# The second half of v's projection among the attention's small products, in chunks 0 to 2 of a sequence

## What is computed

```python
q = relu(split_heads(x @ Wq)) + EPS      # x normalized; 16 heads of 64
k = relu(split_heads(x @ Wk)) + EPS
v = split_heads(x @ Wv)
context = cumsum(einsum('bhnd,bhne->bhnde', k, v), axis=2)
D_inv = 1.0 / einsum('bhnd,bhnd->bhn', cumsum(k, axis=2), q)
attn = einsum('bhnd,bhnde,bhn->bhne', q, context, D_inv)
x = x + attn @ Wo + bo
x = x + down(silu(gate(norm(x))) * up(norm(x)))   # three products with values rounded to an FP4 grid
```

## Time and profile before

| | |
|---|---|
| median of three runs | 1596.24 us (1595.92 to 1596.44) |
| time of the profiled execution | 1595.75 us |
| its span, first to last instruction | 1593.8 us |
| TensorE matmuls, busy | 1574.3 us, 99% of the span |
| VectorE / ScalarE / GpSimd, busy | 1118.9 / 673.1 / 480.5 us |
| granted clock of TensorE, mean | 1.000 of full speed |

### The profile page before, as it was taken

The page is one execution under the profiler, slowest core; times in us unless marked ns, Lnnn a source line. Parts: engine busy times, 40 slices in busy tenths (PEclk is TensorE's granted clock), DMA queues, the critical chain, the costliest instruction groups (busy, mean ns, idle before and its releaser), DMA issues.

```text
span 1593.8 us, 55490 instructions
## 1 busy us (share of the span) xinstructions
PE 1574.3 (99%) x24464; PEld 1483.8 (93%) x24464; DVE 1118.9 (70%) x2438; ACT 673.1 (42%) x1281; POOL 480.5 (30%) x706
## 2 busy tenths in 40 slices
PE   8999999999999999999999999999999999999998
PEld 6889999999999999999999999999999999999998
DVE  8886766676766667666667666676666766666767
ACT  5444344344444434444444443434434444443433
POOL 4332223222233222332232333222322323332233
PEclk9999999999999999999999999999999999999999
DMA  4100000000000000000000000000000000000000
GB/s 161 32 2 16 15 15 6 15 12 16 15 6 15 12 16 16 9 12 15 13 16 15 5 16 12 16 15 15 6 15 12 16 15 6 15 12 16 9 6 18
DMA packets 22013, 26.82 MB, mean 17 GB/s; under 512 B 1808, under 2 KB 20752, under 8 KB 21776
## 3 DMA queue, kind: packets, MB, share of 16 engines
q1 hardware_dynamic: 21776, 23.27, 4.7%
HBM read 14.88 MB, written 8.39 MB: 15 GB/s over the span
## 4 chain that ended last, share of the span: by engine, by line
PE 92%; DVE 4%; issue 2%; DMA 1%; ACT 0%; POOL 0%; SPq 0%; DVEq 0%; POOLq 0%
PE bank L496 65%; PE bank L760 3%; PE bank L629 3%; PE bank L664 3%; PE bank L618 3%; PE bank L805 3%; PE bank L580 3%; PE bank L700 3%; PE bank L727 1%; PE bank L747 1%; PE bank L778 1%; PE bank L602 1%; PE bank L506 1%; DMA qkT<-in_L_attn_Wk 1%; PE bank L739 0%
## 5 line engine op out<-in xcount | busy, mean ns | idle before, releaser
L1380 POOL TENSOR_SCALAR qkT<-qkT 128x512 f32<-128x512 f32 x256 | 190.3, 751 | 267.5 <-ACT qkT L1011 267.3
L1011 ACT ACTIVATE qkT<-bank 128x512 f32<-128x512 f32 x256 | 153.0, 599 | 275.4 <-PE bank L496 223.3
L496 PE MATMUL bank<-xT_hi,wqk_hi 128*128 128x256 f32 x1024 | 213.4, 289 | 0.0
L496 PE MATMUL bank<-xT_hi,wqk_lo 128*128 128x256 f32 x1024 | 203.1, 279 | 0.0
L496 PE MATMUL bank<-xT_lo,wqk_hi 128*128 128x256 f32 x1024 | 203.1, 279 | 0.0
L1350 POOL TENSOR_TENSOR rstd<-var,minus_half 128x1 f32<-128x1 f32 x64 | 35.6, 556 | 430.9 <-DVE var L1664 430.9
L496 PEld LDWEIGHTS bank<-xT_hi,wqk_hi 128*128 128x128 f32 x1024 | 155.2, 188 | 3.4 <-DVE wqk_lo L1467 0.2
L496 PEld LDWEIGHTS bank<-xT_lo,wqk_hi 128*128 128x128 f32 x1024 | 156.0, 188 | 0.0
L496 PEld LDWEIGHTS bank<-xT_hi,wqk_lo 128*128 128x128 f32 x1024 | 155.9, 188 | 0.0
L1467 DVE TENSOR_TENSOR hqT_lo<-bank,hqT_hi 128x512 fp32r<-128x512 f32 x120 | 63.8, 553 | 119.6 <-ACT hqT_hi L1087 119.6
L1467 DVE TENSOR_TENSOR attnT_lo<-bank,attnT_hi 128x512 fp32r<-128x512 f32 (+1 forms) x128 | 88.1, 689 | 60.8 <-ACT attnT_hi L1078 60.4
(11 more groups left out here) (213 smaller groups left out, 3945.5 us busy)
## 6 DMA issues: line engine op xcount, KB each, us to landing
x_in<-in_L_attn_x SPq DMA_DIRECT2D x32, 256.0 KB, 2.8
out<-out_sb SPq DMA_DIRECT2D x64, 128.0 KB, 1.7
qkT<-in_L_attn_Wq SPq DMA_DIRECT2D x1, 1024.0 KB, 8.6
qkT<-in_L_attn_Wk SPq DMA_DIRECT2D x1, 1024.0 KB, 10.7
probs<-in_L_attn_Wv SPq DMA_DIRECT2D x1, 512.0 KB, 3.6
k_tok<-in_L_attn_Wv SPq DMA_DIRECT2D x1, 512.0 KB, 6.5
attn<-in_L_attn_Wo SPq DMA_DIRECT2D x1, 512.0 KB, 12.0
x<-in_L_attn_Wo SPq DMA_DIRECT2D x1, 512.0 KB, 13.0
```

The lines of the kernel that those rows point to most:

```text
L496: at = pe.matmul(dst, lhs_at(kt), rhs_at(kt), start=first and kt == 0, stop=last and kt == k_tiles - 1)
L1011: act.activation(flat(qkT[:, 2 * m:2 * m + 2, :]), bank[bank_of["qk", c, n]][:], ACT.Relu).then_inc(qk_relu, 1)
L1380: pool.tensor_scalar(at, at, QK_EPS, 1.0, ALU.add, ALU.mult).then_inc(qk_ready, 1)
```

## The change

`project_v` and `evacuate_v` get a parameter that says which halves they work on, and `attend` a call that it makes behind the second part of L664, ahead of the queries by state. In chunks 0 to 2 the first half of v is projected where both were, and the second in that new place. In chunk 3 both stay where they were. ScalarE copies the second half behind its square of x. The table of banks is the same. Line numbers behind `attend` are 2 higher in TensorE's program, 4 higher in ScalarE's (5 behind its copy of v) and 5 higher in GpSimd's and VectorE's.

```diff
-            def project_v(b, c, u, t):
+            def project_v(b, c, u, t, parts):
 
-                for n in range(2):
+                for n in parts:
...
-            def attend(b, c, g, u, between):
+            def attend(b, c, g, u, between, amid=None):
...
                         if first:
                             last.then_inc(late_keys_done, 1)
+                if amid:
+                    amid()
...
-                project_v(b, c, u + 1, c % 2)
                 if c < CHUNKS - 1:
-                    attend(b, c, g, u, between)
+
+                    project_v(b, c, u + 1, c % 2, (0,))
+                    attend(b, c, g, u, between, lambda: project_v(b, c, u + 1, c % 2, (1,)))
                 else:
+                    project_v(b, c, u + 1, c % 2, range(2))
                     last_attend(b, c, g, u)
...
-                evacuate_v(c, u + 1, c % 2, 1 - c // 2)
+                evacuate_v(c, u + 1, c % 2, 1 - c // 2, parts=(0,))
                 if g == 2:
                     square_weights(6)
                 if g == 3:
                     square_weights(7)
                 if normed and g != 2:
                     square_x(g - 1)
+                evacuate_v(c, u + 1, c % 2, 1 - c // 2, parts=(1,))
```

More of the change, by code:

```diff
@@ L999, in flat, with evacuate_v @@
                 return t.rearrange("p j t -> p (j t)")
-            def evacuate_v(c, u, t, par, first=0):
-                for n in range(2):
+            def evacuate_v(c, u, t, par, first=0, parts=range(2)):
+                for n in parts:
                     act.wait_ge(v_projected, 4 * u + 2 * t + n + 1)
```

## The result

| | median (runs) | profiled execution | its span |
|---|---|---|---|
| before | 1596.08 us (4 runs, 1594.64 to 1596.44) | 1595.75 us | 1593.8 us |
| changed | 1616.57 us (4 runs, 1615.36 to 1620.28) | 1615.36 us | 1613.4 us |

The ratio of the runs is 1.0138, with a 95% interval of 1.0126 to 1.0150: 22 us. The two medians of the table lie 20.5 us apart, and the two profiled executions 19.6 us; what follows goes by the ratio unless it says otherwise. On the 1596.24 us from which I forecast, the ratio gives 1618.3 us, where I had said 1614 with 1609 to 1617.5. The direction and the boundaries were right, the size 18% too small, and the range ended 0.8 us too low.

A forecast was written before the change was run, and what follows sets the result against it. TensorE's own program was taken as the bound. Boundaries of 0.36 us in 47 chunks, less a wait removed, plus waits brought and the start, made 18.5 us over 1595.75: 1614 us, range 1609 to 1617.5.

The forecast's parts named there:

- the boundaries: v's wide block between two small blocks costs 0.36 us beyond its products, once in each of 47 chunks.
- the range: 1609 (no longer first product) to 1617.5 us (0.25 us from VectorE to TensorE in chunks 2); held 80%.
- The bound: In the steady part TensorE's own program sets the time; other engines count only where a product would wait for them.
- The term I doubted: First wide product behind small ones lasts 0.11 us longer, seen only with 256 columns; bounds 0 and 0.11.
- The estimate of 5.0 us for all boundaries: Two drains of 53 ns at each of 47 places, in place of 16.9 us; a time near 1602 us.
- The wait taken away in chunk 0: L700's 0.11 us wait for VectorE's copy of the state goes, so a chunk 0 costs 0.25 us.
- The waits brought: First L664 waits for `xqT_ready`: 0.12 us late in a chunk 2, just met in chunk 1, covered in chunk 0.
- the sum: 15 chunks each at 0.25, 0.36 and 0.48 us, plus 0.35 and 1.76 at the start: 18.5 us, 1614.2 in all.
- The start: Led by VectorE: g = 1 takes 1.76 us more (six uncovered products and the boundary), g = 0 0.35 us.
- ScalarE and v's bank: In chunks 0 and 2 turn_hq's second part finds v's bank free: no wait, 0.27 us to spare.

The follow-up runs named there:

- e5: Changed kernel with v's second half cut in two, its first two products between the two parts of L664 in chunks 0 to 2: 1631.72 us, ratio to before 1.0221.
- e2: Against the kernel before, only chunk 1 changed: v's second half directly ahead of the q or k projection among the queries by state; ratio 1.0043.
- e7: Kernel before, with nothing between the queries by state and keys by values (L629) ahead of L664 in chunks 1 and 2 too: 1590.88 us, ratio 0.9963.
- e4: Changed kernel with chunk 0's keys by values (L629) between the two parts of L664, as in chunks 1 and 2; ratio to before 1.0138.
- e8: The changed kernel itself measured and profiled once more; ratio to before 1.0133.
- e6: Kernel before, with chunk 1's q or k projection and chunk 2's turn_hq transposes moved behind the late queries: 1595.33 us, ratio 0.9988.

## Why the prediction was right in kind and short in size

- **The bound**: right. Nothing but TensorE's own order and its waits moved the time.
- **The boundaries** (0.11 + 0.11 + 0.09 + 0.05 = 0.36): right. v's block takes 1.60 us, L664 ahead of it 1.15 against 1.04 in chunk 0, and the block behind it 0.62 against 0.58. The term I doubted, the longer first product with 512 columns, was there whole. e5 doubles the added boundaries and costs 0.34 us more in a chunk 1; e2 and e7 have a pair less and give it back. The estimate of 5.0 us for all boundaries, from the Trainium skill's drain of 128 cycles (TensorE: Matmul & The Clock Gate, the step DRAIN), is far too little beside these rows. That TensorE drains at a change of tiling mode, as the Trainium skill's page TensorEngine Tiling (Array Packing) says under Key Properties, agrees with them in kind: each change costs something.
- **The wait taken away in chunk 0** (0.11): the step that failed. "The rest is a wait: L700 reads the state" was a wrong reading. The 0.11 lies inside L664's 64 products, where the second part follows the first part directly; with v's half ahead of L702 it stayed (1.15), and with L629 between the parts (e4) it went. The code has a wait there, for the first part's products (`late_keys_done`). The state's copy was only just ready in time. A chunk 0 cost 0.34 us, not 0.25.
- **The waits brought**: the right semaphore, with the wrong price, and from the same misreading. I took 0.09 from VectorE's end to TensorE's start out of a place that didn't wait. From `xqT_lo` to the first L664 it is 0.25 to 0.26 us (both timelines above; 0.25 also from `wg_lo` in the earlier trace rows, which I had only used for the start and, as a bound, for the range). So L664 starts 1.70 us behind v in chunk 1, where I had called the wait just met, and 1.85 in chunk 2 instead of 1.69. Over the stretch from v's start to what follows the state's early queries this is 5.48 against 5.00 us in chunk 1 (735.66 to 741.14; 726.63 to 731.63) and 5.63 against 5.00 in chunk 2 (766.68 to 772.31, with 757.29 to 762.29 before): 0.48 and 0.63 where the sum had 0.36 and 0.48.
- **The sum again**: 15 x (0.34 + 0.48 + 0.63) = 21.8, plus the start, makes 23.6; the sum had 18.5. Not all of it arrives: from v's start to that of the next chunk the three steps shown cost 0.34, 0.35 and 0.53. The missing 0.1 in chunks 1 and 2 is given back in blocks that the change doesn't touch. In most chunks 1 half of it has a cause. In the one shown, the first transposes of `turn_hq` (L805) started at 735.36 before, 0.05 behind the end of GpSimd's `hq` at 735.31, and took 0.42 us; in the changed kernel `hq` is ready 1.6 us ahead of them, and they take 0.36. In a chunk 2 it is the second gate and up block, which takes 2.07 us in some chunks and 1.99 in others, in either kernel. What decides that I can't say.
- **Luck in the total**: the sum (1614.2) lies only 1.2 us under the changed kernel's profiled execution (1615.36). That is no proof of its terms. They were too small by 0.09, 0.12 and 0.15 us a chunk, and what hid it is what the chunks give back and the 4.0 us of pauses in the profile of before, which the sum took over with its starting point and of which the changed kernel has 0.6.
- **The start**: g = 1 right. L664 started at 49.17 (49.10) after a wait of 2.34 us, and the step grew by 1.75 us where I had said 1.76. For g = 0 I had 0.35, and nothing of it is seen: v of g = 1 started at 45.17 against 45.11, and in e8's profile of the same kernel at 44.82. In between, L629 waited 0.7 us for ScalarE's copy of v in the changed kernel's profile, a wait that I hadn't reckoned with.
- **ScalarE and v's bank**: right, no wait.
- **The range** was too narrow at the top: it allowed for a way of 0.25 us in chunk 2 and "a little" in chunk 1, where that wait costs 15 x 0.12 = 1.8 us, but nothing for the wrong relief in chunk 0 (1.4 us) and nothing for runs with less than the full clock.

## What to carry to other kernels

When TensorE is the bound, count how often its program goes between products on the whole array and products on parts of it. On this kernel each excursion cost some 0.36 us, with six wide products in it or with two, and the gain is in fewer, longer stretches of one kind (e7), not in spreading cover. Before a pause is booked as a wait for another engine, look at where in the block it lies: 0.11 us inside a block of 64 and 0.11 us ahead of the next one look the same in a merged row, and here the mistake spoiled two terms. Then look at how the waiting instruction waits (next section): with several semaphores, the rows speak for waiting last for the one that comes last, which no run here has tried.

## What the runs showed that was not expected

The way from VectorE's end to TensorE's first start is 0.05 us in some places and 0.25 in others. That the first L664 stands behind wide products doesn't explain it. In the changed kernel, L629 waits behind wide products too (step g = 3), and starts 0.06 after `wd_lo` (88.55 + 1.01), where L664 in g = 1, after 2.34 us of waiting, still took 0.25:

```profile
88.55 1.01 DVE L1472 TENSOR_TENSOR wd_lo<-bank,wd_hi 128x512 fp32r<-128x512 f32 x2
...
89.62 0.70 PE L629 MATMUL bank<-v,k_tok 64*64 64x65 f32 x32 [0.51 <-DVE wd_lo L1472]
```

What differs is how each waits. L629's own weight load waits, for one semaphore. Ahead of the first L664 the trace has two instructions that do nothing but wait: one for `k_ready` and `xqT_ready` (L46, in `Banks.take`), one for `probs_ready` (L670). In the chunk 2 above, where VectorE ended at 768.28:

```profile
L46 PEldq EVENT_SEMAPHORE  x1: 51/51/51, 768.3 to 768.3; - x1
L670 PEldq EVENT_SEMAPHORE  x1: 51/51/51, 768.4 to 768.4; - x1
```

They start at 768.32 and 768.43, 51 ns each, the weight load follows at 768.50 and L664 at 768.53. So 0.2 us of the 0.25 go by behind the first of these waits, in others that had long been met. Where the masks come last, which the second instruction waits for, the way is 0.15 (e4's g = 0: masks 32.40, L661 32.55). In e6 L700's weight load waits for the state by itself: 0.05. No run has put the wait for `xqT_ready` last, so what it would give back is an estimate from these rows: the whole 0.13 in a chunk 1 and 0.2 of the 0.28 in a chunk 2.

The granted clock fell in some runs near the start, from full speed to half. e2's profile shows it: each row has a stretch, its length and the busy time of TensorE, its weight loads, VectorE, ScalarE and GpSimd, then the granted clock:

```profile
28.00:38.00 10.00, 8.37 (x195) 6.81 (x188) 9.15 (x14) 3.52 (x7) 3.76 (x4) 0.98 0.27 73
38.00:46.00 8.00, 7.22 (x95) 6.72 (x97) 6.78 (x13) 2.34 (x4) 1.06 (x1) 0.60 0.08 26
```

TensorE was busy for 8.37 of the 10 us from 28 to 38, near the end of which the clock fell, and the mean granted clock is 0.60 from 38 to 46 us, that is mostly at 1.2 instead of 2.4 GHz. The profiles of before and of the changed kernel kept 1.00 there, with TensorE busy for 8.57 and 8.29 of the same 10 us. So the changed kernel was less busy than e2 and didn't fall, and what brings the fall isn't shown.
